# Expert down-projections turned to channel-by-time and summed in one PSUM group, in a Mamba plus mixture-of-experts kernel

## The reference, cut to what matters

```python
h = _layernorm(x, axis=-1) * (1 + ca) + sa
x = x + ga * mamba_fwd_and_bwd(h)                  # 2 directions x 16 states, a scan over 512 steps each
h = _layernorm(x, axis=-1) * (1 + cb) + sb
# w: softmax over the top 2 of 8 gate values per step, zero elsewhere
out = sum over e of (silu(h @ w1[e]) * (h @ w2[e])) @ w3[e] * w[..., e]
out = out + (silu(h @ sw1) * (h @ sw2)) @ sw3      # the shared expert
x = x + gb * out
```

## Time and profile before

| | us |
|---|---|
| median of 3 runs | 2398.07 (2397.0 to 2398.93) |
| the profiled execution | 2398.73 |
| its span, first to last instruction | 2396.9 |

### The profile page before, as it was taken

The page is one execution under the profiler, slowest core; times in us unless marked ns, Lnnn a source line. Parts: engine busy times, 40 slices in busy tenths (PEclk is TensorE's granted clock), DMA queues, the critical chain, the costliest instruction groups (busy, mean ns, idle before and its releaser), DMA issues. The chain is left out here.

```text
span 2396.9 us, 31820 instructions
## 1 busy us (share of the span) xinstructions
PE 2026.4 (85%) x9957; PEld 1283.8 (54%) x9957; DVE 2236.7 (93%) x3546; ACT 1504.6 (63%) x2483; POOL 2021.7 (84%) x1334
## 2 busy tenths in 40 slices
PE   6678988879798888988889798888988888897868
PEld 2445655545565555555545465555555555455544
DVE  4999999999999999999999999999999999999962
ACT  4656666676666666666666666666666666666633
POOL 2777989989898998989989898998989889897855
PEclk7688999999999898999999999998999999999999
DMA  5333433433343333334433343343433333343310
GB/s 148 138 137 124 148 130 128 144 130 136 129 147 134 121 138 134 142 126 145 137 127 132 133 142 134 134 141 118 142 134 140 131 133 137 126 138 131 137 59 27
DMA packets 124060, 312.41 MB, mean 130 GB/s; under 512 B 19700, under 2 KB 46308, under 8 KB 123892
## 3 DMA queue, kind: packets, MB, share of 16 engines
q1 hardware_dynamic: 123892, 310.39, 37.5%
HBM read 303.74 MB, written 6.60 MB: 129 GB/s over the span
## 5 line engine op out<-in xcount | busy, mean ns | idle before, releaser
L504 POOL TENSOR_TENSOR bt<-v,bb 128x1024 f32<-128x1024 f32 x511 | 1205.3, 2360 | 93.8 <-DVE psA L942 72.4
L942 DVE TENSOR_TENSOR_SCAN psA<-psA,bt 128x512 f32<-128x512 f32 x1024 | 1198.1, 1217 | 49.3 <-ACT psA L689 42.4
L689 ACT ACTIVATE psA<-dt,aneg 128x512 f32<-128x512 f32 x1024 | 688.4, 688 | 685.2 <-DVE g L952 684.0
L1209 PEld LDWEIGHTS psY<-ident,g 128*128 128x128 f32 x4096 | 491.6, 147 | 504.5 <-DVE g L952 281.2
L1209 PE MATMUL psY<-ident,g 128*128 128x128 f32 x4096 | 590.1, 286 | 198.1 <-DVE g L952 197.9
L952 DVE TENSOR_TENSOR g<-psA,cb 128x512 f32<-128x512 f32 x1024 | 675.0, 679 | 0.0
L602 POOL TENSOR_TENSOR act<-pf,gf 128x512 f32<-128x512 f32 x288 | 366.8, 1274 | 112.2 <-DVE pf L1046 90.7
L1318 PE MATMUL F<-h2T,w 128*128 128x512 f32 x576 | 334.0, 664 | 112.4 <-DVE pf L1046 110.7
L1364 PE MATMUL F<-w,act 128*128 128x128 f32 x2304 | 298.0, 276 | 4.4 <-POOL act L602 3.1
L1364 PEld LDWEIGHTS F<-w,act 128*128 128x128 f32 x2304 | 276.7, 192 | 14.8 <-POOL act L602 11.0
L1225 PE MATMUL psP<-xnT,wcT 128*128 128x512 f32 x496 | 238.6, 604 | 0.0
(11 more groups left out here) (184 smaller groups left out, 1922.5 us busy)
## 6 DMA issues: line engine op xcount, KB each, us to landing
bb<-bc_rows SPq DMA_DIRECT2D x256, 512.0 KB, 3.7
cb<-bc_rows SPq DMA_DIRECT2D x256, 512.0 KB, 3.6
wB<-w_rows SPq DMA_DIRECT2D x80, 256.0 KB, 4.1
x<-in_L_attn_x SPq DMA_DIRECT2D x16, 256.0 KB, 4.4
out_x<-osb SPq DMA_DIRECT2D x16, 256.0 KB, 4.3
modA<-mod_table SPq DMA_DIRECT2D x15, 192.0 KB, 4.1
w<-in_L_ffn_ew SPq DMA_DIRECT2D x2, 1024.0 KB, 7.2
bc_rows<-xd SPq DMA_DIRECT2D x32, 64.0 KB, 3.0
```

The source lines that it names most:

```text
L504: g.tensor_tensor(bt[:, n % 2, :, :], v[d][:, :, :], bb[:, n // 2 % 2, n % 2, :].unsqueeze(1).broadcast_to([P, NH, T]), ALU.mult).then_inc ...
L689: s.activation(psA[:, half * T:half * T + T], dt_[d][:, half, :], ACT.Exp, scale=aneg[d][:, half, n:n + 1]).then_inc(a_s, 1)
L942: w.tensor_tensor_scan(ah, ah, bt[:, n % 2, half, :][:, order], 0.0, ALU.mult, ALU.add)\
L1209: last = m.matmul(psY[:, half * T + i * P:half * T + i * P + P], g_[:, n % 2, half, i * P:i * P + P], ident[:, :], is_transpose=True, star ...
```

## The change

The down-projection is turned round: `w3` is the stationary operand and `act` (128x512) the moving one, so F2 holds channel by time. Two matmuls per expert take the place of eight. Only two experts stay apart, as `apart = F2 * gate column * weight row` (DVE, 128x512, slots 14 and 16); the other seven are accumulated in one group in F2, with six inputs scaled by POOL (before: five). At the start of the next body ACT copies the group out with the gate column as scale (`fold`), PE turns the three pieces back and adds them up in F1 (`final_turn`, slots 0 and 1), ACT copies F1 to `osb` (slot 1), and POOL adds the residual (slot 2). `fx`, `facc` and `modF` are gone. POOL's `act` product is made two slots after the up-projection (`ACT_LAG = 2`) in six buffers; the last up-projection moves from slot 27 to 29, its `act` to slot 31. The weight rows are broadcast for all eight experts, into three buffers, and their chain begins in slot 10 and no longer in slots 13 and 14; SP waits for it ahead of its `bb` and `cb` loads. The reading of the gate values loses two copies, its exponential goes first in ACT's slot 8, the reciprocal moves from slot 10 to 8 and POOL's weights from 11 to 9. The `zs` of a forward direction move from slots 30 and 31 to the next body's slots 0 and 4, the first backward one from slot 6 to 3. The forward skip term is added in `psY` (slots 8 and 12), and turning back uses transposes. `v` of the backward direction moves from slot 14 to 12, two POOL products of the norm from slot 7 to 4. Some start-up buffers share the place of `apart`.

```diff
-V_SLOT = (30, 14)
-Z_SLOTS, ZS_SLOTS = ((29, 30), (2, 5)), ((30, 31), (6, 6))
+V_SLOT = (30, 12)
+Z_SLOTS = {2: (1, 0), 3: (0, 1), 5: (1, 1)}
+Z_AHEAD_SLOT = 31
+ZS_SLOTS = {0: (0, 0), 3: (1, 0), 4: (0, 1), 6: (1, 1)}
...
-UP_SLOTS = [slot for slot in range(7, 28) if slot not in (9, 10, 22)]
-DOWN_SLOTS = [10, 11, 14, 15, 16, 17, 18, 19, 20, 21, 22, 24, 29, 29, 30, 30, 31, 31]
-SCALED = 4
+UP_SLOTS = [slot for slot in range(7, 30) if slot not in (9, 10, 20, 22, 28)]
+DOWN_SLOTS = [10, 11, 15, 16, 17, 18, 21, 24, 25, 26, 27, 28, 28, 29, 29, 30, 31, 31]
+ACTS = 6
+ACT_LAG = 2
+APART = 2
+PRODUCT_SLOTS = (14, 16)
-TURN_SLOT, ROWS_SLOT = 13, 14
-XS_SLOTS = {16: 4, 18: 5, 20: 6, 22: 7, 24: 8}
+TURN_SLOT = 10
+ROW_SLOTS = {0: 11, 1: 11, 2: 11, 3: 14, 4: 16, 5: 17, 6: 19, 7: 21}
+XS_SLOTS = {14: 3, 16: 4, 18: 5, 21: 6, 24: 7, 26: 8}
+FOLD_SLOT, FINAL_SLOT, COPY_SLOT, OUT_SLOT = 0, 1, 1, 2
...
# POOL, one expert product
-                k = up_at(slot - 1)
+                k = up_at(slot - ACT_LAG)
...
-                    g.tensor_tensor(act[:, k // 2 % 3, k % 2, :], pf[:, k % 2, :], gf[:, k % 3, :], ALU.mult)\
+                    wait(pool, down_s, at - ACTS + 1)
+                    g.tensor_tensor(act[:, k % ACTS, :], pf[:, k % 2, :], gf[:, k % 3, :], ALU.mult).then_inc(act_s, 1)
...
# ACT
+            def fold(fb):
+                act_e.wait_ge(down_s, UPS * fb + UPS)
+                s.activation(foT, F2[:, :], ACT.Copy, scale=modC[:, 2:3]).then_inc(F2_free, 1)
+            def copy_out(fb):
+                act_e.wait_ge(fin_s, fb + 1)
+                wait(act_e, out_d, 16 * fb)
+                s.activation(osb[:, :, :], F1[:, :], ACT.Copy).then_inc(fin_free, 1)
...
             def body(b, scan, ffn, last):
                 for slot in range(STEPS):
                     nxt = slot + 1
+                    if slot == FOLD_SLOT and b >= 2:
+                        fold(b - 2)
                     if slot == 0 and ffn:
                         keep_y(b - 1, 1)
...
# DVE
-                    for i in range(NT):
-                        w.scalar_tensor_tensor(facc[:, i, :], F2[:, i * D:i * D + D],
-                                               wts[:, i, ORDER[e]:ORDER[e] + 1], facc[:, i, :],
-                                               ALU.mult, ALU.add).then_inc(facc_s, 1)
+                w.scalar_tensor_tensor(apart[:, p, :], F2[:, :], modC[:, 2:3], wB[:, n % ROWS, :],
+                                       ALU.mult, ALU.mult).then_inc(F2_free, 1)
...
# PE
+                for k in downs_at(slot):
+                    if k <= 2 * APART and k % 2 == 0:
+                        pe.wait_ge(F2_free, free + DOWN + k // 2)
+                    pe.wait_ge(act_s, UPS * fb + k + 1)
+                    m.matmul(F2[:, :], w3[:, ORDER[k // 2], k % 2, :], act[:, k % ACTS, :],
+                             start=(k <= 2 * APART and k % 2 == 0), stop=(k < 2 * APART and k % 2 == 1 or k == UPS - 1))\
+                        .then_inc(down_s, 1)
```

More of the change, by code:

```diff
@@ L74, in downs_at, with z_order, row_expert @@
 def downs_at(slot):
-    return [divmod(k, 2) for k, at in enumerate(DOWN_SLOTS) if at == slot]
-ORDER = [NX] + list(range(NX))
+    return [k for k, at in enumerate(DOWN_SLOTS) if at == slot]
+def z_order(b, d, half):
+    return 4 * b + 2 * d + half if b == 0 else 4 * b + d + 2 * half
+def row_expert(idx):
+    return ORDER[idx if idx < APART else idx + 1]
 def adaln_mamba_moe(nc, t, out):
@@ L417, in body @@
                         rows_out(b + 1, 0)
+                    if ffn:
+                        scales(b - 1, slot)
                     if slot % 2 == 0:
@@ L449, in scales @@
                     sp.dma_start(w_dram, wtsT[:, :]).then_inc(wrow_out, 16)
[L450 to L456, removed]
+                for idx, at in ROW_SLOTS.items():
+                    if slot == at:
+                        if idx == 0:
+                            sp.wait_ge(wrow_out, 16 * fb + 16)
+                        scale_row(fb, idx)
             def early(b, scan, ffn, last):
@@ L645, in body @@
                             bmul(STEPS * b + nxt, 0, 0)
-                    if slot == 0 and not (isinstance(b, int) and b < 2):
+                    if slot == OUT_SLOT and b >= 2:
                         output(b - 2)
@@ L861, in body @@
                         keep_y(b, 0)
+                    if ffn and slot == GATE_SLOT + 1:
+                        act_e.wait_ge(gate_s, GATES * (b - 1) + GATE_D)
+                        s.activation(ge[:, :], gd[:, :], ACT.Exp).then_inc(ge_s, 1)
                     if ffn:
@@ new lines, in skip, with turn @@
+            def skip(d, half):
+                for i in range(NT):
+                    m.matmul(psY[:, half * T + i * P:half * T + i * P + P], u[d][:, half, i * P:i * P + P],
+                             diag[:, d, half, :], start=False, stop=False, skip_group_check=True)
+            def turn(bank, d, half, opened):
+                for i in range(NT):
+                    last = m.matmul(bank[:, i * P:i * P + P], acc[d][:, half, i, :], ident[:, :], is_transpose=True,
+                                    start=not opened, stop=(not opened or i == NT - 1))
+                return last
@@ new lines, in final_turn @@
+            def final_turn(fb, slot):
+                if slot == FINAL_SLOT - 1:
+                    pe.wait_ge(F1_free, UPS * fb + UPS)
+                    pe.wait_ge(F2_free, FREES * fb + DOWN + APART)
+                    for p in range(APART):
+                        for i in range(NT):
+                            m.matmul(F1[:, i * P:i * P + P], apart[:, p, i * P:i * P + P], ident[:, :],
+                                     is_transpose=True, start=(p == 0 and i == 0), stop=False, skip_group_check=True)
+                if slot == FINAL_SLOT:
+                    pe.wait_ge(F2_free, FREES * fb + FREES)
+                    for i in range(NT):
+                        last = m.matmul(F1[:, i * P:i * P + P], foT[:, i * P:i * P + P], ident[:, :],
+                                        is_transpose=True, start=False, stop=True, skip_group_check=True)
+                    last.then_inc(fin_s, 1)
@@ L1263, in side @@
                     wait(pe, pP_free, post_piece(b, half))
-                    skip_and_turn(psP, 0, half).then_inc(pP_full, 1)
+                    turn(psP, 0, half, False).then_inc(pP_full, 1)
+                if post_f and slot in SKIP_SLOTS:
+                    skip(0, SKIP_SLOTS.index(slot))
                 if prep_f is not None:
@@ L1283, in ffn_side @@
                         pe.wait_ge(acc_s, 4 * fb + 4)
[L1284 to L1287 removed]
+                    wait(pe, F2_free, FREES * fb + POSTB + half)
+                    m.matmul(F2[:, :], diag[:, 1, half, :], u[1][:, half, :], start=True, stop=False)
+                    turn(F2, 1, half, True).then_inc(F2_full, 1)
                 if slot == TURN_SLOT:
@@ L1403, in body @@
                         sum_y(step - 1, 4 * b - 2, N - 1)
+                    if b >= 2 and slot in (FINAL_SLOT - 1, FINAL_SLOT):
+                        final_turn(b - 2, slot)
+                    if slot == Z_AHEAD_SLOT and scan_ and not last:
+                        project_z(b + 1, 0, 0)
                     if ffn:
```

286 lines of the change are left out of this document (126 added, 160 removed).

## The result

The changed kernel takes 2444.45 us (median of 4 runs, 2443.78 to 2448.93), the kernel before 2398.5 on the same chip (2397.0 to 2399.29). The ratio is 1.0196 with a 95% interval of 1.0179 to 1.0214: slower by 46 us. Forecast were 2405 and a range of 2358 to 2424. The kernel became slower, as the likeliest case said, but by 46 us and not by 7.

What follows compares the result with a forecast made beforehand. DVE bounds the kernel (busy 1936.1 of 1993.0 us). From 2398.7: 15 bodies x (-3.65 + 0.35) = -49.5, 14 seams x (1.0 + 3.3) = +60.2, tail -2, small corrections: 2405 us, range 2358 to 2424.

Steps and rivals of the forecast that it cites:

- DVE's work, -2.83 busy: DVE, every sample: 4.03 us of work removed and 1.20 added for two products; busy time falls by about 43 us.
- The wait of 0.36 for `bt` and that of 0.23 for PE are gone.: DVE's waits per sample, for `bt` behind POOL's late weight row and for PE at slots 17 and 18, both vanish.
- POOL, middle slots, +0.35, bounds 0 and 1: Reordered POOL work makes the products for the scans of slots 12 and 14 slightly late: +0.35 us per sample.
- Rival 3: POOL decides from slot 12 to 19, about 1.5 us per sample: 2428; part of the 0.15 chance above 2420.
- POOL in the seam, 1.0: Slots 29 to 0: `act` behind `dt` delays each `bt`, so DVE waits 1.0 us for slot 0's.
- The chain of slot 1, 3.3: Last `act` delays last down, `sum_y`, `keep_y` and exponentials; DVE waits 3.3 us at slot 1, 2.4 if PE is fast.
- at nothing, covered by that idle: PE's twelve turning passes and four split skip matmuls fill its 19 us idle per sample; cost nothing, otherwise about 1 us.
- the same, so nothing: On PE, a down of 2 passes of 512 lasts as long as 8 of 128 columns: no cost.
- Removed: three experts in four pieces: DVE drops the weighted expert additions, 1.03 us from one start to the next: 3.09 us saved per sample.
- The slow clock: After over 4 us idle, PE runs the last down mostly at 1.2 GHz, taken as 2.03 us.
- Rival 1: `act` 17 comes early enough, so only DVE's work counts: 2346, or up to 2390 with some seam wait; chance 0.27.
- Rival 2: The last down runs at 2.4 GHz, 14 x 0.9 us less: 2392; part of the forecast's own range, chance 0.58.

Runs made afterwards that it cites:

- the mended kernel: The changed kernel with last two expert products one slot behind, tanh ahead of `keep_y` in slot 16, downs last in slots 26 and 27: 2350.28 us, 0.9809.

## Why the prediction was wrong, point by point

In short: of the 2.95 us per sample that the forecast missed, 2.0 are waits for `tf`. They come from two terms that were not followed to the next wait, the full saving of the removed expert additions and the moved downs at nothing. Another 0.8 is the gate sum (`final_turn` at nothing, on a late and slow PE), and 0.6 is `bt`, in the places and for the reason that were forecast.

*DVE's work, -2.83 busy.* Right: -2.83 per sample, 45.9 us in all against 43 (13 instructions less per sample, not 12). One price was too low. The product of three factors takes 741 ns and 0.66 to the next start (1274.48 to 1275.14), not 0.60: 0.12 per sample. It was taken from two rows that have no scalar per partition. The small terms made up for it.

*The sample's length.* The 142.36 and the 0.3 by which the one sample read was said to exceed the mean come from the stretch with the shorter last sample. Full samples take 142.71, so the 1.7 us taken off the sum for it had no ground.

*"The wait of 0.36 for `bt` and that of 0.23 for PE are gone."* Both right. POOL's wait for the weight row, 30.1 us in the whole run before, is 4.5.

*POOL, middle slots, +0.35, bounds 0 and 1.* Within its bounds, but more than twice its value: 1.98 - 1.22 = 0.76 of waits for `bt` outside slot 0, two of 0.4 ahead of the scans of slots 12 and 14, the places that were named. Rival 3, that POOL decides from slot 12 to 19, did not happen; no wait for `bt` there passed the 0.5 that was named.

*POOL in the seam, 1.0.* Right: 1.22, for the reason given (shown by the run with half expert 16 alone). Slot 0's scan starts 8.77 after slot 30's, where 8.78 were worked out; the 0.2 between the waits is the empty slot's own wait for the exponential, which the forecast counted as part of its length and which now lies under the other.

*The chain of slot 1, 3.3.* Right in each link and in what ends it. One term was mis-sized: "`sum_y`, 1.0 to 1.25" was read in a stretch where PE was busy, yet it runs right behind a down that was priced on the slow clock. It took 1.91, and the wait was 3.93. The sum should have used one clock for both. The other ACT waits fell by more than forecast (to 5.49 - 3.93 = 1.56 a sample from 2.47), so that the line as a whole came out at +3.02 against +3.07. That agreement is by two errors that cancel.

*`final_turn`, "at nothing, covered by that idle".* This step failed too. The forecast followed the chain to the exponentials and stopped there, but PE's queue goes on. Behind the late down and the sum stand the turning passes (eight in 1.91 on the slow clock) and other work, and only then the transposes for `acc`: +0.79. PE's 19 us of idle per sample lay elsewhere; here it has none from the last down to these transposes. With PE warm the same passes are there and the wait is gone, and so it is with the last product early. So it takes the late down and the slow clock together; no run leaves `final_turn` out, and what its passes alone cost is not shown.

*A down is "the same, so nothing".* This is the other step that failed in PE's part. It compared lengths (1.13 against 1.95 for twice as many) and not places. The list of down slots moved, downs came to stand ahead of the projection for `dt` in slots 26 and 27, and the tanh two steps on came 0.57 late twice: the two slots are 0.91 per sample longer than before. The run with the downs last gave 0.87 of it back.

*"Removed: three experts in four pieces", 3.09.* The step that failed most, as its saving was counted without what stood under it. In slot 15 DVE's 1.03 us stood over a chain through PE and ACT that had nothing to spare. The prediction asked for such cover in the seam and not in the middle, and quoted the very row, 1246.05, whose removal uncovers it. Of the 1.03 nothing came in the sample shown (5.23 us from `pf` to `pf` in both kernels). The run with `keep_y` behind the tanh gave back 1.21 per sample in this slot.

*The sum.* Forecast +1.00 per sample, measured +3.95. The 2.95 that miss, in each of 14 samples, are 41 us, and the miss of the whole is 39.5 (2444.45 against 2405). The terms at the ends were small and roughly right: the tail is 3.3 shorter where 2 were forecast.

*The slow clock.* After 4.68 us of idle the down takes 2.07 us, with 1.12 in the run in which PE was kept busy, and the granted clock behind it is 0.56. The rule of the Trainium skill in "TensorE: Matmul & The Clock Gate", Part 1, that an idle TensorE falls to 1.2 GHz, agrees with this trace. The forecast applied it to the down alone.

*The rivals.* Rival 1, 2346 if only DVE's work counts, is what the mended kernel reaches within 5 us (2350.28): the saving was priced well, and its condition, that nothing else is late, had to be built. That the two numbers are so close is in part luck, as `bt` is still late and the start is 4.4 us shorter than before. Rival 2 (2392 with PE warm) was too low: warm, the kernel takes 2421.73, since the waits in slots 16, 27 and 28 stay, and 2.16 of slot 1's. The range's upper end failed because it was built of more of the known wait and of rival 3, with no room for a chain not looked at.

## What to carry to other kernels

Work taken off the bounding engine is also a gap filled less: for each removed instruction, go to the next instruction there that needs another engine, follow its chain back to this engine, and read how much it had to spare; that is the most that the removal can save. Follow a late chain through every queue to the last instruction that waits for it, with one clock for all of its PE work. When instructions only change their places in an in-order queue, list what stands behind each new place: here three re-orderings that remove no work were worth 94 us, twice the change's whole saving.

## What the runs showed of the hardware

- Eight 128x128 transposes of float32 with `is_transpose` took 1.04 us with PE kept busy (the run with five extra matmuls) and 1.91 us on the slow clock (the changed kernel): here they follow the granted clock as a matmul does (1.12 and 2.07 for two of 512 columns).
- Five matmuls that do nothing, put into an idle of 4.7 us, made the kernel 21 to 23 us faster, and the down and the sum behind them 1.82 us shorter in a seam.
- A product with two tensor operands and a scalar per partition (128x512, PSUM and SBUF) takes 741 ns on DVE (`apart`), the same operation with a constant scalar 678 (`pf`).
- The slow clock can end sooner or later behind the same instructions: in two successive samples of the run with the downs last it was granted 0.80 and 0.52 in the same four microseconds behind the last down, and the second sample lasted 1.1 us longer (145.63 and 144.54).
